# Graph-attention and edge-network kernel: attention shares spread by broadcast loads, more chunks staged ahead, and scatters shifted between two edge stages

## What is computed

```
h = relu(layernorm(x))
x_l = h @ W_l + b_l;  x_r = h @ W_r + b_r        # 4 heads of 32; every node also has a loop edge
e = att . leaky_relu(x_l[src] + x_r[dst])        # per edge and head
x = x + bias + segment_sum(softmax_by_dst(e) * x_l[src])
h = relu(layernorm(x))
W = (ssp(edge_attr @ Wf1 + bf1) @ Wf2 + bf2) * edge_weight
agg = segment_sum((h @ W_in)[dst] * W, by src)   # ssp is softplus - log 2
x = x + ssp(agg @ Wo1 + bo1) @ Wo2 + bo2
```

## Time and profile before

| | before |
|---|---|
| median of 3 runs | 3064.7 us (3061.18 to 3067.32) |
| profiled execution: its own time | 3060.97 us |
| profiled execution: span from first to last instruction | 3059.1 us |
| mean granted TensorE clock | 0.924 |
| busy share of the span: PE, DVE, ACT, POOL | 81%, 74%, 63%, 61% |
| DMA | 557.94 MB, mean 182 GB/s |

### The profile page before, as it was taken

How to read it: one execution, slowest core, us unless ns; L and a number is a source line. 1 busy time by engine, 2 the same in 40 slices (tenths; PEclk the granted TensorE clock), 3 DMA queues, 4 the chain that set the end, 5 groups by cost and what they waited for, 6 DMA issues and landing times. The chain is left out here.

```text
span 3059.1 us, 59638 instructions
## 1 busy us (share of the span) xinstructions
PE 2481.3 (81%) x16702; PEld 1699.7 (56%) x16702; DVE 2262.0 (74%) x6291; ACT 1940.3 (63%) x4383; POOL 1870.8 (61%) x1633
## 2 busy tenths in 40 slices
PE   5988997999999998988677767777777777488877
PEld 4666663444444444445555555555555555377776
DVE  6787775788788877776777777777777777367666
ACT  4888886666566665552455555555555555289887
POOL 3455774377777777761488888888888888600000
PEclk8999999999999999987799898988999988799999
DMA  7899984254444544442456555555556556689998
GB/s 210 282 297 293 290 281 165 73 158 157 153 155 152 162 145 150 148 122 93 103 112 124 111 117 117 115 120 110 121 114 119 116 111 121 171 336 426 426 414 305
DMA packets 366956, 557.94 MB, mean 182 GB/s; under 512 B 141123, under 2 KB 218295, under 8 KB 341698
## 3 DMA queue, kind: packets, MB, share of 16 engines
q1 hardware_dynamic: 269890, 448.38, 43.9%
q0 software_dynamic: 96960, 108.35, 18.8%
HBM read 323.98 MB, written 241.26 MB: 185 GB/s over the span
## 5 line engine op out<-in xcount | busy, mean ns | idle before, releaser
L716 POOL DMA_INDIRECT sum_dram<-b_sum,b_at x392 | 639.9, 1632 | 141.9 <-issue 112.9
L634 POOL DMA_INDIRECT a_xs<-in_x,index x352 | 349.4, 993 | 114.1 <-issue 98.5
L641 POOL DMA_INDIRECT a_xd<-in_x,index x352 | 350.1, 995 | 107.3 <-issue 100.9
L704 POOL DMA_INDIRECT x_dram<-b_xo,sidx x294 | 312.6, 1063 | 106.6 <-issue 93.2
L1651 PE MATMUL bank<-b_rows,b_same 128*128 128x128 bf16 x4704 | 292.1, 224 | 0.0
L1684 PE MATMUL bank<-wo,f_ssp_out 128*128 128x128 f32 x1568 | 229.0, 292 | 69.7 <-DVE f_ssp_out L1200 68.0
L1254 ACT ACTIVATE d_n<-d_x,stat_d_shift,stat_d_rstd 128x128 f32<-128x128 f32 x686 | 283.7, 486 | 0.2 <-DVE stat_d_shift L752 0.2
L1651 PEld LDWEIGHTS bank<-b_rows,b_same 128*128 128x128 bf16 x4704 | 277.2, 101 | 0.0
L1684 PEld LDWEIGHTS bank<-wo,f_ssp_out 128*128 128x128 f32 x1568 | 204.7, 204 | 87.5 <-DVE f_ssp_out L1200 81.2
L1461 PE MATMUL bank<-ident,d_n 128*128 128x128 f32 x1184 | 191.8, 287 | 70.2 <-DMA d_n<-sum_dram 38.9
L1507 PE MATMUL bank<-wl,turned 128*128 128x128 f32 x1568 | 232.5, 292 | 11.0 <-ACT turned L1251 9.3
(11 more groups left out here) (233 smaller groups left out, 6256.3 us busy)
## 6 DMA issues: line engine op xcount, KB each, us to landing
d_x<-in_x SPq DMA_DIRECT2D x196, 256.0 KB
x_dram<-d_x SPq DMA_DIRECT2D x196, 256.0 KB
out<-d_x SPq DMA_DIRECT2D x49, 1024.0 KB, 10.4
sum_dram<-zero SPq DMA_DIRECT2D x48, 1024.0 KB
d_x<-x_dram SPq DMA_DIRECT2D x45, 1024.0 KB, 14.2
d_n<-sum_dram SPq DMA_DIRECT2D x25, 1024.0 KB, 11.9
x_end_dram<-a_xo SPq DMA_DIRECT2D x98, 256.0 KB
b_x<-x_end_dram SPq DMA_DIRECT2D x98, 256.0 KB
```

Of the source, the lines that this page charges most:

```text
L634: pool.indirect_dma_start(a_xs[t % DEPTH][:, j * F:(j + 1) * F], None, x, column(t, j)).then_inc(gathered[t % GSEM], 16)
L641: pool.indirect_dma_start(a_xd[t % DEPTH][:, j * F:(j + 1) * F], None, x, column(t, TILES + j)).then_inc(gathered[t % GSEM], 16)
L704: pool.indirect_dma_start(x1_dram, bass.IndirectOffsetOnAxis(ap=sidx[s][:, j:j + 1], axis=0), b_xo[s][:, j * F:(j + 1) * F], None, bounds_ ...
L716: pool.indirect_dma_start(sum_dram, bass.IndirectOffsetOnAxis(ap=b_at[s][:, j:j + 1], axis=0), b_sum[s][:, j * F:(j + 1) * F], None, compu ...
```

## The change

- Shares: the matmul with `pick` goes. Once per pack SP stores `p_beta` (32 rows of 2 KB) to `beta_dram`, waits until that has landed, and then loads for every chunk four rows, each broadcast to 32 partitions, into `a_beta` (two buffers). The keep flags are loaded with their sign turned (`gate_dram`), so `a_gate` = (`a_beta` - 1) * (-keep), and the transposes of `a_o` use `neg_ident`: the same values as before. `p_beta` has one buffer instead of two, and `shares` waits for the store of the pack before.
- Order: on VectorE the back (`a_gate`, `a_pv`, scan) stands behind `a_u` instead of ahead of it, and `shares` ahead of `a_xo`; on TensorE the transposes of `a_o` stand at the end of a step. The freed bank 7 takes the backs of odd chunks, bank 6 those of even ones.
- Staging: 16 staged chunks instead of 10, in four slots instead of two (`SPARE`). Only 20 chunks (`FIRST`) are gathered within the node stage; slots 20 to 23 are filled after it. The remaining gathers are 464 instead of 512, and end at chunk 80.
- Scatters: even chunks scatter two row tiles in the first edge stage (`EARLY = (2, 1)`), so POOL has 147 scatters there instead of 98, and 245 instead of 294 in the second; there, every other chunk has two scatters instead of three.

```diff
-EARLY = (1, 1)
+EARLY = (2, 1)
-STAGED = 10
+STAGED = 16
+FIRST = 20
+SPARE = DEPTH - FIRST
...
-                    sp.dma_start(a_keep[c % 2][:, :], keep_dram[c:c + 1, :].broadcast_to([P, C])).then_inc(keep_loaded[c % 2], 16)
+                    if c % PACK == 0:
+                        sp.wait_ge(rows_dve, by_dve(c // PACK, "beta"))
+                        sp.sem_inc(sync_step, 1)
+                        sp.dma_start(beta_dram[c // PACK, :, :], p_beta[:, :]).then_inc(beta_stored, 16)
+                        sp.wait_ge(beta_stored, 16 * (c // PACK + 1))
+                        sp.sem_inc(sync_step, 1)
+                    for h in range(HEADS):
+                        p = 8 * h + c % PACK
+                        sp.dma_start(a_beta[c % 2][h * HC:(h + 1) * HC, :], beta_dram[c // PACK, p:p + 1, :].broadcast_to([HC, C])).then_inc(spread[c % 2], 16)
+                    sp.dma_start(a_keep[c % 2][:, :], gate_dram[c:c + 1, :].broadcast_to([P, C])).then_inc(keep_loaded[c % 2], 16)
...
             def gather_stage(i, j):
-                slot = DEPTH - 1 - i % 2
-                if j == 0 and i >= 2:
-                    pool.wait_ge(stage_stored, 32 * (i - 1))
+                slot = DEPTH - 1 - i % SPARE
+                if j == 0 and i >= SPARE:
+                    pool.wait_ge(stage_stored, 32 * (i - SPARE + 1))
...
-            ahead += [(gather, t, h) for t in range(DEPTH) for gather in (gather_src, gather_dst) for h in range(2)]
+            ahead += [(gather, t, h) for t in range(FIRST) for gather in (gather_src, gather_dst) for h in range(2)]
...
+            for t in range(FIRST, DEPTH):
+                for h in range(2):
+                    gather_src(t, h)
+                    gather_dst(t, h)
...
-                until = min(len(rest), -(-len(rest) * (t + 1) // (NC - LAG - 8)))
+                until = min(len(rest), -(-len(rest) * (t + 1) // (NC - LAG - 6)))
...
-                if b >= 2:
-                    dve.wait_ge(spread, PACK * (b - 1))
-                dve.scalar_tensor_tensor(out=p_beta[b % 2][:, :], in0=p_up[:, :], scalar=1.0, in1=p_run[:, 0:C],
+                if b >= 1:
+                    dve.wait_ge(beta_stored, 16 * b)
+                dve.scalar_tensor_tensor(out=p_beta[:, :], in0=p_up[:, :], scalar=1.0, in1=p_run[:, 0:C],
...
-                    dve.scalar_tensor_tensor(out=a_gate[:, :], in0=bank[7][:, :], scalar=1.0, in1=a_keep[s][:, :],
+                    dve.scalar_tensor_tensor(out=a_gate[:, :], in0=a_beta[s][:, :], scalar=-1.0, in1=a_keep[s][:, :],
                                              op0=ALU.add, op1=ALU.mult)
-                    dve.tensor_tensor(a_pv[:, :], bank[7][:, :], a_xs[c % DEPTH][:, :], ALU.mult).then_inc(weighted, 1)
+                    dve.tensor_tensor(a_pv[:, :], a_beta[s][:, :], a_xs[c % DEPTH][:, :], ALU.mult).then_inc(weighted, 1)
...
-                    pe.matmul(bank[7][:, :], pick[:, n * P:(n + 1) * P], p_beta[b % 2][:, :], start=True, stop=True).then_inc(spread, 1)
-                    if c >= 1:
-                        pe.wait_ge(x1_ready, c)
+                    to = bank[6 + c % 2]
+                    if c >= 2:
+                        pe.wait_ge(x1_ready, c - 1)
```

More of the change, by code:

```diff
@@ L182, in gnn @@
         a_keep = two("a_keep", [P, C], BF16)
+        a_beta = two("a_beta", [P, C])
         a_gate = sb("a_gate", [P, C])
@@ L194, in gnn @@
         p_up = sb("p_up", [PR, C])
-        p_beta = two("p_beta", [PR, C])
+        p_beta = sb("p_beta", [PR, C])
         p_col = sb("p_col", [PR, 8])
@@ L588, in _ @@
             pool.wait_ge(pool_setup, 3)
-            pool.affine_select(out=pick[:, :].rearrange("p (c h k) -> p c h k", c=PACK, h=HEADS),
-                               in_=pick[:, :].rearrange("p (c h k) -> p c h k", c=PACK, h=HEADS), compare_op=ALU.not_equal, fill=-1.0, base=0,
-                               pattern=[[-1, PACK], [-8, HEADS], [0, HC]], channel_multiplier=1)
+            pool.affine_select(out=pick[:, :].rearrange("p (c h) -> p c h", c=PACK),
+                               in_=pick[:, :].rearrange("p (c h) -> p c h", c=PACK), compare_op=ALU.not_equal, fill=1.0, base=0,
+                               pattern=[[-1, PACK], [-8, HEADS]], channel_multiplier=1)
             pool.affine_select(out=lower_f[:, :].rearrange("p (j c) -> p j c", j=TILES),
@@ L616, in _ @@
             pool.wait_ge(index_ready, 3)
[L617 removed]
+            pool.wait_ge(store_setup, 144)
             def column(t, n):
@@ L1026, in step_a @@
                     dve.tensor_tensor(a_dif[:, :], a_hd[t % (LAG + 1)][:, :], bank[0][:, :], ALU.subtract).then_inc(differed, 1)
-                if back:
-                    s = c % 2
-                    dve.wait_ge(spread, c + 1)
-                    dve.wait_ge(keep_loaded[s], 16 * (c // 2 + 1))
-                    dve.scalar_tensor_tensor(out=a_gate[:, :], in0=bank[7][:, :], scalar=1.0, in1=a_keep[s][:, :],
-                                             op0=ALU.add, op1=ALU.mult)
-                    dve.tensor_tensor(a_pv[:, :], bank[7][:, :], a_xs[c % DEPTH][:, :], ALU.mult).then_inc(weighted, 1)
-                    dve.wait_ge(weighted, c + 1)
-                    if c >= 1:
-                        dve.wait_ge(sum_scan, c)
-                    if c >= 2:
-                        dve.wait_ge(out_turned, c - 1)
-                    dve.tensor_tensor_scan(a_o[s][:, :], a_gate[:, :], a_pv[:, :], a_o[1 - s][:, C - 1:C] if c else 0.0,
-                                           ALU.mult, ALU.add).then_inc(sum_scan, 1)
                 if packed and phase == 0:
@@ L1054, in step_a @@
                                              op0=ALU.add, op1=ALU.max).then_inc(edge_max, 1)
+                if back:
+                    s = c % 2
+                    dve.wait_ge(spread[s], 64 * (c // 2 + 1))
+                    dve.wait_ge(keep_loaded[s], 16 * (c // 2 + 1))
+                    dve.scalar_tensor_tensor(out=a_gate[:, :], in0=a_beta[s][:, :], scalar=-1.0, in1=a_keep[s][:, :],
+                                             op0=ALU.add, op1=ALU.mult)
+                    dve.tensor_tensor(a_pv[:, :], a_beta[s][:, :], a_xs[c % DEPTH][:, :], ALU.mult).then_inc(weighted, 1)
+                    dve.wait_ge(weighted, c + 1)
+                    if c >= 1:
+                        dve.wait_ge(sum_scan, c)
+                    if c >= 2:
+                        dve.wait_ge(out_turned, c - 1)
+                    dve.tensor_tensor_scan(a_o[s][:, :], a_gate[:, :], a_pv[:, :], a_o[1 - s][:, C - 1:C] if c else 0.0,
+                                           ALU.mult, ALU.add).then_inc(sum_scan, 1)
                 if packed and phase == 1:
@@ L1060, in step_a @@
                     sums_a(t + LEAD)
+                if packed and phase == 3:
+                    shares(b)
                 if back:
@@ L1065, in step_a @@
                         dve.wait_ge(early_scattered[s], 16 * EARLY[s] * ((c - 4) // 2 + 1))
-                    dve.tensor_tensor(a_xo[c % 4][:, :], bank[6][:, :], a_xd[c % DEPTH][:, :], ALU.add).then_inc(x1_ready, 1)
+                    dve.tensor_tensor(a_xo[c % 4][:, :], bank[6 + c % 2][:, :], a_xd[c % DEPTH][:, :], ALU.add).then_inc(x1_ready, 1)
                 if t % 2 and t + LEAD < NC:
@@ L1076, in step_a @@
                     carry_den(b)
-                if packed and phase == 3:
-                    shares(b)
             for t in range(LEAD):
@@ L1576, in step_a @@
                     pe.matmul(bank[4][0:PR, 0:8], same_head[:, :], p_own[:, :], start=True, stop=True).then_inc(row_mm, 1)
-                if back:
-                    pe.wait_ge(sum_scan, c + 1)
-                    for j in range(TILES):
-                        last = pe.matmul(bank[6][:, j * F:(j + 1) * F], a_o[c % 2][:, j * P:(j + 1) * P], ident[:, :],
-                                         start=False, stop=(j == TILES - 1))
-                    last.then_inc(out_turned, 1)
                 if front:
@@ L1596, in step_a @@
                     turn_dst(t + 1)
+                if back:
+                    pe.wait_ge(sum_scan, c + 1)
+                    for j in range(TILES):
+                        last = pe.matmul(bank[6 + c % 2][:, j * F:(j + 1) * F], a_o[c % 2][:, j * P:(j + 1) * P], neg_ident[:, :],
+                                         start=False, stop=(j == TILES - 1))
+                    last.then_inc(out_turned, 1)
             turn_src(0)
```

37 lines of the change are left out of this document (19 added, 18 removed).

## The result

The changed kernel takes 3096.99 us (median of 4 runs, 3092.91 to 3101.01), the kernel before in the same comparison 3062.94 us (4 runs, 3052.7 to 3067.32). The ratio is 1.0116 with a 95% interval of 1.0086 to 1.0146: it is slower by some 1.2%. The prediction was 3044 us, its range 2994 to 3088.

What follows compares the result with a forecast made beforehand. POOL was taken to bound both edge stages, TensorE pacing the first until POOL's slack ran out. Node stage +10, first edge stage +17, tail -4, second edge stage -44 gave -21 on 3060.97: 3040, as median 3044; range 2994 to 3088.

Steps and rivals of the forecast that it cites:

- First edge stage, the other engines: hidden behind POOL: First edge stage: VectorE's circle takes 66 us per pack against POOL's 69, so removing the spreading matmul is worth nothing there.
- what would make it wrong: Sign against the prediction: POOL idles in the first edge stage, or the time between second-stage adds falls to 4.5 us.
- the rival of the round trip: First edge stage: the shares' store and loads stall VectorE 8 us or more per pack, 3081 us in all; chance 0.17.
- node stage: Stage before the first edge stage: more staged chunks load the DMA engines further, +10 us, bounds 0 and 20.
- POOL, +17: First edge stage: -7 us for fewer instructions, 19 for waits beside two-SBUF-operand `a_gate` and `a_pv`, 5 for the first packs.
- tail: First edge stage after POOL's last gather: two banks let TensorE make a base early, -4 us, bounds -15 and +6.
- second edge stage: Last scatters: 49 fewer, the next add following after some 4.95 us instead of 5.84, -44 us, bounds 65 and 28 gained.
- the rival with 120 us: First edge stage: POOL waits for the end of `a_gate`, `a_pv` and scan, 120 us instead of 19, 3145 in all; chance 0.09.

## Why the prediction was wrong, step by step

**The step that failed is "First edge stage, the other engines: hidden behind POOL".** It gave VectorE's circle 66 us per pack, POOL 69, "so POOL stays the bound, by 3 us per pack". The circle took 73.3, and POOL waited for it. The text had named this as what would make it wrong. In its sum VectorE's busy time, 53.3 per pack, was right (562.62 / 786.0 x 73.3 = 52.5). The idle time was 12.5 in the forecast and 18.6 in the trace, in these three waits alone (2.2 more are in shorter gaps):

- At `a_u`: 6.8 + 2 = 8.8 forecast, 119.0 / 9.55 = 12.5 measured. The forecast took 1.69 us, from the start of the matmul on `a_dif` to `a_u`, in four of seven steps. That way was sized about right (1.81 in the median), but the matmul itself starts 0.30 us behind the end of `a_dif`, and the wait comes in nearly every step: 2.1 to 2.9 us in the mean in the three steps of a pack without pack work, 0.8 to 1.8 in the four others. What ends it is ScalarE, where `a_ns` (1.65 us), `a_us` and `a_xs` stand in one queue, and `a_ns` begins within 0.3 us of `a_dif`, behind `stat_e_shift` in odd steps and behind `a_hd` in even ones. In 52 of 67 steps `a_us` ends after the matmul, but by 0.13 us in the median and 0.57 at most, so the two ways are nearly equally long; no run shortened either of them.
- At `a_dif`: 0 forecast, 39.4 / 9.55 = 4.1 measured. The 1.63 us at `a_dif` stood in the earlier trace rows; the sum left it out. Nearly all of it is in even steps, behind the statistics (37.5 of 40.0 us). It had been larger before (75.7 us), so that one could have seen in the trace of before that VectorE waits for `a_hd` in most steps.
- At `a_gate`: 3.7 forecast, 2.0 per pack in the total (19.5 / 9.55), 2.8 each time it occurs. The store and the loads were sized well: from the end of `shares` to the first `a_gate` 7.1 to 8.2 us, where 7.9 were forecast. So the rival of the round trip was the wrong mechanism, and that its time, 3081, was the nearer one is luck: giving the round trip a step more gained 13 us.

The experiment with the order undone shows that the new order, and so the circle, is the cause: it gives back 56 of the 84 us between the changed kernel and the one with staging and scatters alone (55 of 82 by the ratios). With POOL nearly full again, the other terms of the sum come out near their size in its trace (of an execution 9 us below that kernel's median): first `a_xo` +5.0 (node stage, +10 forecast), from there to the last gather +14.2 (POOL, +17), tail -3.8 (-4), second edge stage -34.8 (-44).

**Second edge stage: mechanism right, size off by a cause that was not in the list.** 44 us were forecast with the next add 4.95 us behind the last. With staging and scatters alone it is 4.95, and first to last add takes 1112 us instead of 1164, 52 less: the distance before was 5.98 in the mean, not the 5.84 of the one row that the sum took, and 1.03 x 49 = 50. In the changed kernel it was 5.39, and the stage gained 36.5 us. The 0.44 us x 49 = 21 between them are the price of the DRAM tensors' place, as the two experiments on it show.

**Node stage: +10, between 0 and 20.** The stage itself ended 3.6 us later, and the first `a_xo` came 9.7 later. In the ten kernels of the study with 16 staged chunks, the changed one among them, the last add into `d_x` starts between 472.3 and 484.0 us, 478 in the mean, against 473.0: 5 us, half the term and within its bounds, with a spread larger than itself. The DMA share at 100 to 200 us rose to 0.97, not 1.01, and POOL's eight waits for a staging slot are gone; a single wait of 4.4 us is left, at a store.

**POOL, +17.** The 5 instructions fewer and the 19 us of waiting beside `a_gate` and `a_pv` could not show in the changed kernel, where POOL had idle time. With the order undone POOL is nearly full again: 606.43 us busy for 572 instructions between 576 and 1362 us, 1.060 each, against 601.57 / 581 = 1.035 with the spreading matmul. 0.025 x 586 = 15 us, where 19 were forecast. The two kernels differ in the loads as well, so I sorted POOL's indirect DMAs of this stretch by the operation of VectorE in which they start. With the spreading matmul 80 start within `a_gate` or `a_pv`, and none took over 1.02 us; with the two SBUF operands 83 do, 57 of them took over 1.1 us, the longest 1.51. Above the median of 0.946 these carry 17.7 us instead of 1.4, so the term was right in mechanism and size. One of them, with the order undone:

```profile
916.60 0.69 DVE L1048 SCALAR_TENSOR_TENSOR a_gate<-a_beta,a_keep 128x512 f32<-128x512 f32 x1
...
916.89 1.21 POOL L651 DMA_INDIRECT a_xs<-in_x,index  x1 [0.30 <-issue]
```

None was held to the end of all three operations, each ended at least 0.35 us before the scan did: the rival with 120 us did not come. The Trainium skill, page "SBUF — State Buffer", section "Who interferes with whom", says that VectorE operations with two SBUF inputs contend with GpSimd's reads. The trace agrees, with the 57 of 83 against none of 80.

**Tail: -4, between -15 and +6.** From the last gather to the last `a_xo` it took 120.2 us instead of 110.3, outside the bounds. The order is behind most of this too. Of the 9.9 us, 8.7 lie in the steps after the last gather that still have a front (44.9 us to the last `a_dif` instead of 36.2), which is the circle again. With the order undone the tail is 106.5 us, 3.8 less than before, as forecast. Why it is 114.0 with staging and scatters alone isn't shown.

## What to carry to other kernels

Where one engine leads the next circle by a few per cent only, that circle has to be summed wait by wait, and each wait that the trace of before already shows on it belongs in the sum. Before work is moved out of the gap between two operations, measure the gap from the end of the one to the start of the other in the steps where it is bare, along every way between them: here the way over TensorE's matmul and the way through ScalarE's queue are nearly equally long. And test edits that share an engine alone and together: the second scatters alone lost 0.5%, and on top of the staging gained as much.

## What the runs showed of the hardware that was not expected

The time of a broadcast load changed when the tensors in DRAM were shifted by 1017856 bytes: over the kernels, `b_w` landed in 3.7 to 4.1 us (median of 98 loads) at the one place and in 4.6 to 4.8 at the other. In three pairs of kernels that was worth 15 to 17 us of the whole (0.5%), as the adds to another tensor landed later too.

TensorE's granted clock was low in a step behind a wait. Its two levels here are 1.2 and 2.4 GHz, and a share between 0.5 and 1 is a mean of both. Granted clock and busy time in three short stretches of the changed kernel: the step of a pack's first `a_gate`, the one behind it, and a later one:

```profile
870.00:881.00 11.00, 7.24 (x27) 4.06 (x27) 6.17 (x18) 2.35 (x6) 6.42 (x6) 0.76 0.85 254
881.00:889.00 8.00, 8.00 (x20) 3.32 (x18) 3.17 (x6) 5.27 (x13) 5.92 (x7) 0.69 0.58 189
889.00:901.00 12.00, 11.23 (x57) 6.57 (x56) 9.57 (x30) 4.95 (x12) 8.17 (x7) 1.00 0.72 211
```

In the first, TensorE was busy for 7.24 of 11 us, and VectorE waited 3.2 us for the shares. Then TensorE stood idle for 3.76 us ahead of the transposes of `a_o`, and these and what follows ran at the lower level until about 886 us. In the second stretch the matmul on `a_dif` took 1.91 us, where at 2.4 GHz it takes 1.02, and VectorE's wait at `a_u` was 3.78 us instead of 2.20:

```profile
877.51 2.08 PE L1612 MATMUL bank<-neg_ident,a_o 128*128 128x128 f32 x8 [3.76 <-DVE a_o L1076]
...
883.92 1.91 PE L1589 MATMUL bank<-a_dif,wl 128*128 128x512 f32 x2
...
886.50 0.75 DVE L1062 SCALAR_TENSOR_TENSOR a_u<-bank,cols,a_xs 128x512 f32<-128x512 f32 x1 [3.78 <-ACT a_xs L1344]
...
893.09 1.02 PE L1589 MATMUL bank<-a_dif,wl 128*128 128x512 f32 x2
```

Between 600 and 1300 us the granted clock was 0.94 in the changed kernel and 0.97 before, so part of the longer steps is TensorE's own: as an estimate at most 0.03 x 73.3 = 2.2 of the 7.5 us per pack, if TensorE's time counted in full. With the order undone the clock is hardly higher (0.95), and a pack takes 67.3 us.
